# A routing table written with its slots innermost, and the first block's low halves ahead of the remaining low weight rows

## The reference

```python
scores = jnp.maximum((x @ gate_W + gate_b) / TEMP, EPS)     # 1250 x 8
p = jax.nn.softmax(scores, axis=-1)
_, topk_idx = jax.lax.top_k(p, K)                           # K = 2
topk_mask = jax.nn.one_hot(topk_idx, E, dtype=p.dtype).sum(-2) > 0
w = jnp.maximum(p, W_THRES)
w_gather = jnp.take_along_axis(w, topk_idx, axis=-1)
w = w / w_gather.sum(-1, keepdims=True)
comb = jnp.where(topk_mask, w, jnp.zeros_like(w))
y = jnp.einsum('bsd,edf->bsef', x, expert_W) + expert_b
out = jnp.einsum('bsef,bse->bsf', y, comb) / K
```

## Time and profile before

| | |
|---|---|
| median of three runs | 1229.18 us (1228.38 to 1230.64) |
| span of the profiled execution | 1227.3 us; its own time is not given beside the span |
| TensorE matmuls busy | 1180.4 us (96%) |
| VectorE busy | 753.9 us (61%) |
| ScalarE, GpSimd busy | 308.7 us (25%), 447.5 us (36%) |
| mean DMA rate | 127 GB/s |

### The profile page before, as it was taken

One profiled execution on the slowest core, in us unless ns is written; L12 is line 12 of the kernel. 1 busy time (PEld: TensorE's weight loads), 2 busy tenths in 40 slices (PEclk: granted clock), 3 DMA queues, 4 the chain that ended last, 5 costly groups with the idle time before them and its releaser, 6 DMA issues.

```text
span 1227.3 us, 16308 instructions
## 1 busy us (share of the span) xinstructions
PE 1180.4 (96%) x5799; PEld 991.5 (81%) x5799; DVE 753.9 (61%) x1511; ACT 308.7 (25%) x416; POOL 447.5 (36%) x434
## 2 busy tenths in 40 slices
PE   6999999999999999999999999999966999999996
PEld 5798888888788988889887888888855788888884
DVE  7999522454334677777667437998488822643434
ACT  2412112132111111111012123333251611432223
POOL 3950687878785000000000006224232443444343
PEclk9999999999999999999999999999966999999998
DMA  6111442843311322211046652242276965785754
GB/s 210 36 35 35 127 116 70 271 138 80 101 44 37 93 91 91 91 54 59 33 133 193 195 156 62 100 184 105 100 280 230 364 130 85 206 273 114 201 90 75
DMA packets 91031, 156.08 MB, mean 127 GB/s; under 512 B 14786, under 2 KB 45244, under 8 KB 90836
## 3 DMA queue, kind: packets, MB, share of 16 engines
q1 hardware_dynamic: 75556, 129.76, 31.3%
q0 software_dynamic: 15408, 25.44, 11.7%
HBM read 112.95 MB, written 42.04 MB: 126 GB/s over the span
## 4 chain that ended last, share of the span: by engine, by line
PE 91%; DVE 7%; issue 1%; ACT 1%; DMA 0%; DVEq 0%; POOL 0%; ACTq 0%; POOLq 0%
PE ps L1646 28%; PE ps L1647 28%; PE ps L1648 28%; PE ps L1777 2%; DVE e_lo L1471 2%; PE ps L1820 2%; PE ps L1891 2%; PE ps L1737 1%; DVE tok_w L1585 1%; PE ps L1690 1%; DVE stats L1065 0%; DVE xn_lo L1093 0%; DVE y L1616 0%; ACT lt_hi L989 0%; DVE xt_lo L1058 0%
## 5 line engine op out<-in xcount | busy, mean ns | idle before, releaser
L715 POOL DMA_INDIRECT tab_d<-val_i,addr_i x160 | 203.9, 1274 | 109.1 <-issue 109.1
L1646 PE MATMUL ps<-e_hi,lt_hi 128*128 128x512 f32 x368 | 148.0, 402 | 2.8 <-DVE e_lo L1471 2.1
L730 POOL TENSOR_TENSOR att_part<-att 128x640 f32<-128x640 f32 x10 | 15.8, 1581 | 363.0 <-PE ps L1648 349.7
L1648 PE MATMUL ps<-e_hi,lt_lo 128*128 128x512 f32 x368 | 144.1, 392 | 0.0
L1647 PE MATMUL ps<-e_lo,lt_hi 128*128 128x512 f32 x368 | 143.9, 391 | 0.0
L1646 PE MATMUL ps<-xt_hi,q_hi 128*128 128x416 f32 (+1 forms) x384 | 142.0, 370 | 0.0
L1647 PE MATMUL ps<-xt_lo,q_hi 128*128 128x416 f32 (+1 forms) x384 | 135.3, 352 | 0.0
L1648 PE MATMUL ps<-xt_hi,q_lo 128*128 128x416 f32 (+1 forms) x384 | 134.9, 351 | 0.0
L1304 DVE TENSOR_TENSOR cnt<-ps,cnt 128x256 f32 x208 | 87.2, 419 | 39.3 <-PE ps L1777 24.2
L819 POOL DMA_INDIRECT out<-y,row_put x46 | 74.0, 1608 | 89.5 <-ACT y L1023 57.1
L1646 PEld LDWEIGHTS ps<-e_hi,lt_hi 128*128 128x128 f32 x368 | 69.5, 189 | 23.1 <-DVE e_lo L1471 8.9
(11 more groups left out here) (293 smaller groups left out, 2670.7 us busy)
## 6 DMA issues: line engine op xcount, KB each, us to landing
e_raw<-in_L_ffn_expert_W SPq DMA_DIRECT2D x64, 512.0 KB, 9.8
acc<-in_x SPq DMA_DIRECT2D x18, 512.0 KB, 8.3
w_raw<-in_L_mix_w_key SPq DMA_DIRECT2D x16, 512.0 KB, 4.2
h_d<-hs SPq DMA_DIRECT2D x18, 256.0 KB, 2.0
q_in<-q_d SPq DMA_DIRECT2D x9, 512.0 KB, 5.3
xm<-in_x SPq DMA_DIRECT2D x18, 256.0 KB
h_in<-h_d SPq DMA_DIRECT2D x9, 512.0 KB, 6.4
mix_d<-xm SPq DMA_DIRECT2D x18, 256.0 KB
```

What stands on the lines that cost most here:

```text
L715: nc.gpsimd.indirect_dma_start(out=tab_d, out_offset=bass.IndirectOffsetOnAxis(ap=addr_i[0:EP, j:j + 1], axis=0), in_=val_i[0:EP, j:j + 1] ...
L1646: nc.tensor.matmul(o, lh, rh, start=(k == 0), stop=False)
L1648: return nc.tensor.matmul(o, ll, rh, start=False, stop=(k == last_k))
```

## The change

At line 1585 the table is written in the order of its layout: pairs outermost, the 29 slots innermost, so that the output is 29 neighbours at a time. The operand `tok_s` is then read across its layout, with a step of 20 elements; `w_part` is repeated over the slots. The numbers computed are the same. Further down, both halves of `block_lo` of the first block come ahead of all four remaining rows of `expert_lo`, where before the second half stood behind row 4.

```diff
--- before.py
+++ after.py
@@ -1582,7 +1582,8 @@
             link(V.tensor_tensor(w_rest[:, :], w_rest[:, :], w_part[:, 1, :], ALU.subtract))
             link(V.tensor_copy(w_part[:, 2, :], w_rest[:, :]))
             for j in range(3):
-                last = V.tensor_tensor(tok_w[:, :, j, :].rearrange("p t s -> p s t"), tok_s[:, :, :], over_slots(w_part[:, j, :]), ALU.mult)
+                last = V.tensor_tensor(tok_w[:, :, j, :], tok_s[:, :, :].rearrange("p s t -> p t s"),
+                                       w_part[:, j, :].unsqueeze(2).to_broadcast([P, 2 * NT, NSLOT]), ALU.mult)
             last.then_inc(s_wtab, 1)
             dve.wait_ge(s_padt, 1)
             V.tensor_tensor(last_c[:, :, :], io16[:, 0:NSLOT].unsqueeze(1).to_broadcast([P, NE, NSLOT]),
@@ -1590,10 +1591,9 @@
             link(V.tensor_tensor(pad_r[:, :, :], io16[:, :].unsqueeze(1).to_broadcast([P, NE, P]),
                                  pad_at[:, :].unsqueeze(2).to_broadcast([P, NE, P]), ALU.is_equal))
             V.tensor_tensor(pad_c[:, :, :], last_c[:, :, :], pad_t[:, :].unsqueeze(2).to_broadcast([P, NE, NSLOT]), ALU.mult).then_inc(s_pad, 1)
-            block_lo(0, 0)
-            expert_lo(0, range(FIRST_LO, MB + 1))
-            block_lo(0, 1)
-            expert_lo(0, range(MB + 1, KB))
+            for g in range(2):
+                block_lo(0, g)
+            expert_lo(0, range(FIRST_LO, KB))
             dve.wait_ge(s_padp, 1)
             link(V.tensor_tensor(slot_f[:, :], ps[:, 6, 64:64 + NSLOT], slot_f[:, :], ALU.add))
             for h in range(NH):
```

## The result

The changed kernel takes 1224.79 us in the median of 13 runs (1223.13 to 1229.20), the kernel before 1229.37 in 13 runs beside it (1227.50 to 1230.92). The ratio is 0.9965 with a 95% interval of 0.9956 to 0.9974: 4.3 us faster by the ratio (3.2 to 5.4; the two medians lie 4.6 us apart), more than the 0.2% that can be told from nothing. The forecast was 1224.9. The profiled execution took 1225.22 us, with a span of 1223.4, where 1223.0 was forecast.

The account below looks back on a forecast made before the run. TensorE was taken to bound the kernel end to end, standing still during the table write. VectorE's -8.0 + 3.6 - 0.1, about -4.5, met a -4.3 gather ceiling: span 1223.0 plus 1.9 gives 1224.9 us, range 1222.9 to 1227.9.

Parts of the forecast that it names:

- the line through two stepped four-byte reads: Table write, line 1585: lines 1531 and 1180 give 1.83 ns per element plus 145 ns fixed, 3.6 us for three instructions.
- The tail of the slow writes: In `last_c`, behind the table write: part of its 0.61 us looked like slow writes finishing, worth up to 0.2 us more.
- The first expert matmul: TensorE's opening of the expert blocks: forecast to move from 936.14 to about 931.9 us, with VectorE still setting the start.
- whole possible cost: Reordered low halves, first block: at the high clock throughout, the last `e_lo` row would be 0.4 us late; edit priced at nothing.
- TensorE as the next bound of the start: First expert block: with the table at 1.35 us instead of 3.6, TensorE would bound at 931.4, only 0.5 us more.
- The ceiling of the second gather: Second block's transposes: the gather, landing at 938.86, does not move, so its 4.3 us of slack caps the gain.
- should come no later: TensorE's clock: working nearly without pause from 927.31, its rise should come no later against the first block's start.
- The softening: Second gather: if the slow table write lengthened its GpSimd instruction, landing comes 0.7 us sooner and the ceiling is 5.0.
- Rival (d): GpSimd's chain: small loads taking 9.3 us delay the third gather, costing 0.6 to 1.5 us; chance 0.15.
- (a): Table write: the price only moves from write to read, so the time stays at 1229.2; chance 0.10.
- (b): Line 1585: a stepped two-byte read is dearer than the stepped write; at 6 ns the kernel takes 1232.1; chance 0.03.
- (c): TensorE's clock rises later in the first block, the gain falling from 4.2 to 0.9, halfway 2.6; chance 0.16.

Follow-up runs that it names:

- single prices: Changed kernel plus seventeen lone VectorE products of 580 elements at its start, dense or stepped: stepped two-byte write 2.77 us, read 1.12 to 1.20.
- order alone: Kernel before with only the new order of low halves, old table write kept: 1229.07 us, ratio 0.9996 to the kernel before.
- table alone: Kernel before with only the new table write, old order of low halves kept: 1225.53 us, ratio 0.9971 to the kernel before.
- one fill: Changed kernel plus nine unread 512-column matmuls in TensorE's wait for the first gather: 1224.07 us, ratio 0.9961 to the kernel before.
- dense layout: Changed kernel with slot tables and slot numbers laid out slots innermost, so neither table read nor write steps: 1224.39 us, 0.9962 to the kernel before.
- three fills: Changed kernel plus 8, 9 and 14 unread matmuls in TensorE's three routing waits: 1226.98 us, ratio 0.9974 to the kernel before.
- the fill and the early small loads: Changed kernel with nine fill matmuls and two small loads ahead of GpSimd's row_of wait: 1223.99 us; with expert 2's loads after the second gather, 1222.96.
- small loads early: Changed kernel with the two small loads issued ahead of GpSimd's wait for row_of: 1225.71 us, ratio 0.9966 to the kernel before.

## Why the prediction was right

- The table write: 3.6 us forecast from the line through two stepped four-byte reads, 3.38 measured, 1181 ns an instruction against 1204. The single prices have two-byte reads at 1.12 to 1.20 us. That the read would be far cheaper than the write was right; that the size came out so close is partly luck, for the line does not hold for the four-byte reads it was drawn through. A four-byte read of 580 elements at 348 bytes took 1.51 us, not 1.20, and one of the line's two rows (line 1180) is a reduction, not a product.
- The tail of the slow writes in `last_c`, "up to 0.2 us", was there: 0.61 to 0.40.
- The first expert matmul: 931.9 forecast, 931.86 measured; but the table write began 0.25 us later in this execution, so the gain up to there was 4.53 us where I took 4.2. Of the 0.3 us between them, 0.2 is the table write (3.38 for 3.6); the rest is that I had counted full durations, and neighbouring instructions overlap a little (`last_c` began at 929.19, before the table's end at 929.28).
- The reorder at nothing: shown by the order alone. The 0.4 us given as its "whole possible cost", the last row of `e_lo` being late at the high clock, is no cost of the edit: four rows and two halves stand ahead of that point in either order. The wait is real and small, 0.2 us, and the same in the old order (table alone: a step of 0.45 us between two matmuls at 935.13 and 935.58, for 0.23) and in the new one (one fill: 0.44).
- TensorE as the next bound of the start, with 0.5 us to gain from a cheaper table: the dense layout gained 0.75 us there, with TensorE as the bound, and lost as much ahead of it.
- The ceiling of the second gather was right as a mechanism and not what stopped this execution. The step "TensorE would get there just behind the landing" came out at 0.9 us behind it, where 0.1 was forecast: half because the gather landed at 938.5, not 938.9, half because TensorE came at 939.4, not 939.0, the clock having risen 1.0 us later in the block. That the rise "should come no later" against the block's start failed in this profile. Where the clock rose earlier, a wait of 0.5 to 0.9 us was there (table alone, dense layout, one fill, three fills), but not with the fill and the early small loads.
- So the profiled gain is 4.53 us at the start less some 0.5 us lost to the clock, 4.1 at the third transposes (46.53 against 42.41). In other executions the same 4.5 meets the gathers instead: the table alone, waiting for both, has 3.3 left there, one fill 4.5 with a wait of 0.9. That the forecast total was hit, with the ceiling as its reason, is partly luck.
- The softening, 0.7 us from a faster GpSimd instruction, was wrong as a reason: it still took 1.74 us beside the faster table (1.86 before), and with the slow table write and the new order 1.80. The landing, 8.6 us for 9.3, is not the change's doing either, since the order alone has 8.7. That a shorter instruction goes with an earlier landing is borne out in the dense layout: 1.02 us, and 8.1 to land.
- Rival (d), the third gather, is real, but with another mechanism than given: the small loads landed in 5.1 us, not 9.3; the wait, 1.5 us in the table alone, comes where the loads of expert 3 start close to the gather or ahead of it, and only where TensorE is early enough.
- Rivals (a) and (b) are refuted by the 1181 ns at line 1585 and by the single prices, (c) by size: the rise was 1.0 us later in this profile and cost 0.5 us, not several; in the order alone it was 2.4 us later, so a later rise looks like a matter of the execution more than of the change; with one profile of most kernels that is not shown.

## What to carry to other kernels

Where a small two-byte tensor must be turned over on VectorE, let the read take the step, not the write, if the step is over 4 bytes (at 4 bytes both sides cost nearly the same, 0.76 and 0.80 us). For four-byte data it makes no difference at 348 bytes. Before a stretch is shortened, list for each transfer behind it whether its trigger moves with the stretch: those whose trigger stays become the ceiling, and those that move can overtake them. Filling a wait to lift the clock is only safe with less work than the shortest wait at the low clock, and no fill here was shown to make the kernel faster.

## What the runs showed of the hardware that was not expected

- A product of 580 bf16 elements on VectorE took 0.46 us dense, 0.80, 1.44 and 2.08 us with its output at steps of 4, 8 and 12 bytes, 2.67 at 60 and 2.77 at 174; with the same steps in its input (4 to 174) 0.76, 0.76, 0.92, 1.12 and 1.20. In four-byte data, steps of 348 bytes took 1.5 us on either side, and a step of 8 bytes nothing (0.76, as dense).
- TensorE's clock rose from 0.5 us before to 4.3 us after the first expert matmul in kernels whose TensorE work ahead of it is the same (table alone, changed kernel, small loads early), and at 3.2 and 5.7 us in the two with the slow table write. Each microsecond of that within the block is worth 0.47 us: the second transposes of the order alone and of the kernel before stand 1.1 us apart for it, those of the changed kernel and the table alone 0.85, with the wait for the gather in between.
- With three fills the clock rose to 2.4 GHz after the first, held through the second (nine matmuls, done at 918.16) and fell back to 1.2 GHz at about 921.3, when TensorE had stood still for 2.9 us and had just begun the products of 29 columns.
- An indirect gather of 128 rows landed in 4.3 to 5.1 us alone or well ahead of the loads that followed it, and in 8.0 to 9.3 beside eight loads of 512 KB. The loads of expert 2 moved away brought the second gather from 8.6 to 5.0.
